# A fused four-layer image kernel: a shorter chain in the scan, fewer products in the global mixer, mode mixing with the modes stationary, and pieces of the output moved between two stages

## What is computed

```python
# layer 0: a = rfft2(x)[:, :, :32, :32];  two blocks of modes, each mixed over the 64 channels by complex weights
blk1 = _complex_matmul_2d(a, fw1)      # einsum bixy,ioxy->boxy, fw1 and fw2 of shape (64, 64, 32, 32, 2)
blk2 = _complex_matmul_2d(a, fw2)
out = irfft2(out_ft);  return relu(out @ W + b + out)
# layer 1: channels 0..31 windowed attention, channels 32..63 the global mixer, then a projection
fre = rfft2(xc); amp = abs(fre); pha = angle(fre)
amp_fea = amp * amp_w + amp_b;  pha_fea = pha * pha_w + pha_b
out = abs(irfft2(complex(amp_fea * cos(pha_fea) + 1e-08, amp_fea * sin(pha_fea) + 1e-08) + 1e-08))
# layer 2: the 16 x 16 lowest modes of fftn mixed, and back
# layer 3: for each of 1024 masked points the best context point by cosine, then a scan in raster order
def step(prev, inp):                   # prev: (8, 256) here
    mn, bst, mx = inp
    prev_n = prev / (norm(prev) + EPS)
    d_ad = maximum(sum(mn * prev_n), 0.0)
    cur = (d_ad * prev + mx * bst) / (d_ad + mx + EPS)
    return cur, cur
```

## Time and profile before

| what | us |
|---|---|
| median of 3 runs (lowest, highest) | 16272.47 (16264.12, 16278.23) |
| the profiled execution's own time | 16263.63 |
| its span in the trace | 16261.9 |
| mix_modes0 | 608 to 1287 |
| global_mixer with its last store | 6171 to 9204 |
| point_rows | 11751 to 12300 |
| select_points | 12303 to 13225 |
| coherent_scan | 13230 to 15920 |

### The profile page before, as it was taken

The page is one execution under the profiler, slowest core; times in us unless marked ns, Lnnn a source line. Parts: engine busy times, 40 slices in busy tenths (PEclk is TensorE's granted clock), DMA queues, the critical chain, the costliest instruction groups (busy, mean ns, idle before and its releaser), DMA issues. The chain is left out here.

```text
span 16261.9 us, 298044 instructions
## 1 busy us (share of the span) xinstructions
PE 11005.2 (68%) x109058; PEld 8114.0 (50%) x109058; DVE 9523.5 (59%) x20093; ACT 7395.5 (45%) x13170; POOL 4376.3 (27%) x3172
## 2 busy tenths in 40 slices
PE   8696667999999997999999899867715940000002
PEld 3493224777777776888888788532212410000001
DVE  3113445777777775666666433244465668888883
ACT  5211224777777774555554322433313544444440
POOL 0002344565655651111111255200005730000001
PEclk9757888999999998999999999988857975555555
DMA  6676673111111110111111499978896620000007
GB/s 258 174 145 203 215 243 115 41 43 39 42 42 42 42 42 31 61 44 42 52 53 42 145 363 364 325 238 358 364 376 206 183 76 9 10 10 9 10 10 290
DMA packets 1289991, 2177.92 MB, mean 134 GB/s; under 512 B 98836, under 2 KB 941988, under 8 KB 1221668
## 3 DMA queue, kind: packets, MB, share of 16 engines
q1 hardware_dynamic: 853124, 1613.43, 29.9%
q10 hardware_dynamic: 415008, 488.75, 9.2%
q0 software_dynamic: 20608, 58.22, 1.3%
HBM read 1370.06 MB, written 790.14 MB: 133 GB/s over the span
## 5 line engine op out<-in xcount | busy, mean ns | idle before, releaser
L731 POOL TENSOR_TENSOR la_s<-la_s,la_mx 128x512 f32<-128x512 f32 x2048 | 2094.3, 1044 | 1457.0 <-DVE la_mx L690 1456.7
L1928 PE MATMUL fp_tp<-fp_idn,fp_f 128*128 128x128 f32 x512 | 89.4, 344 | 2967.4 <-DMA fp_f<-ft 2950.0
L1928 PEld LDWEIGHTS fp_tp<-fp_idn,fp_f 128*128 128x128 f32 x512 | 77.8, 180 | 2979.6 <-issue 2761.2
L770 ACT ACTIVATE la_et<-la_pt 128x512 f32<-128x512 f32 x2048 | 1118.8, 600 | 737.6 <-PE la_pt L602 737.6
L602 PE MATMUL la_pt<-la_idn,la_s 128*128 128x128 f32 x8192 | 1152.0, 285 | 219.7 <-POOL la_s L731 219.2
L690 DVE TENSOR_REDUCE la_mx<-la_s 128x16 f32<-128x1024 f32 x1024 | 1243.6, 1215 | 17.7
L682 DVE TENSOR_TENSOR la_s<-la_ps,la_post 128x2048 f32<-128x2048 f32 x512 | 1168.4, 2282 | 31.5 <-PE la_ps L588 31.3
L602 PEld LDWEIGHTS la_pt<-la_idn,la_s 128*128 128x128 f32 x8192 | 904.2, 144 | 335.4 <-issue 235.3
L1801 ACT ACTIVATE cs_junk<-cs_num 8x256 f32<-8x256 f32 x1024 | 427.0, 417 | 1323.9 <-DVE cs_num L1862 1090.5
L895 PE MATMUL gm_xp<-gm_fws,gm_y 128*128 128x258 f32 x4096 | 962.8, 389 | 52.8 <-ACT gm_ri L968 52.8
L1232 PE MATMUL pj_pp<-pj_pw,pj_at 128*128 128x256 f32 x4096 | 926.4, 379 | 0.0
(11 more groups left out here) (272 smaller groups left out, 27499.7 us busy)
## 6 DMA issues: line engine op xcount, KB each, us to landing
f_xt<-in_x SPq DMA_DIRECT2D x128, 1024.0 KB, 8.0
i_xr<-in_x SPq DMA_DIRECT2D x64, 2048.0 KB
x<-pj_o SPq DMA_DIRECT2D x64, 2048.0 KB, 10.1
f_xt<-x SPq DMA_DIRECT2D x128, 1024.0 KB, 13.8
i_xr<-x SPq DMA_DIRECT2D x64, 2048.0 KB, 14.4
x<-i_xo ACTq DMA_DIRECT2D x64, 2048.0 KB, 14.5
mx_fw<-in_L_conv_fw SPq DMA_DIRECT2D x32, 2048.0 KB
x1l<-i_xo ACTq DMA_DIRECT2D x128, 512.0 KB, 10.7
```

The lines of the kernel that those rows point to most:

```text
L731: nc.gpsimd.tensor_tensor(sv, sv, mb, ALU.subtract).then_inc(s_sub, 1)
L770: nc.scalar.activation(et[:, k % RT].rearrange("p h n -> p (h n)"), t_bank(S, i)[:, :, :].rearrange("p h n -> p (h n)"), ACT.Exp).then_inc ...
```

## The change

The four parts are independent of each other.

**1. `EARLY` 8 to 3.** point_rows keeps 6 pieces an image, select_points gets 18; nothing else in the two functions changes.

```diff
-EARLY = 8
+EARLY = 3
```

```diff
-    NK = 2
...
+    NK = 4
...
+                def load(t):
...
+                    for half, src in zip(halves, (fw1, fw2)):
+                        for q in range(3):
+                            sp.dma_start(a[half, j, q, :, :], modes[:, q, :, kx].rearrange("b i n -> i b n")).then_inc(s_a[j], 16)
+                        sp.dma_start(fw[half, j, :, :], src[:, :, t * NK:(t + 1) * NK, :, :].rearrange("i o x y r -> i o (x y r)"))\
...
+                def mix(n):
...
+                    for s in range(SLOTS):
+                        for r in range(2):
+                            for g in range(G):
...
+                                for f, half in enumerate(halves):
+                                    last = nc.tensor.matmul(mp[g * 32:g * 32 + M, n % 2, f, s * C:(s + 1) * C],
+                                                            a[half, j, 1 - r:3 - r, :, x * NM0 + ky].rearrange("p q b -> p (q b)"),
+                                                            fv[half, :, x, ky, r], start=(r == 0), stop=(r == 1))
...
+                def turn(n):
...
+                            last = nc.tensor.matmul(tz[n % 2][half, s * G * M:(s + 1) * G * M],
+                                                    zs[:, n % 2, f, s * C:(s + 1) * C], sel[:, :], start=True, stop=True)
...
-                                    last = nc.tensor.matmul(mp[n % 2][f][half, ky * 2 * B:(ky + 1) * 2 * B],
-                                                            fv[half, :, x, ky, r], rhs, start=(r == 0), stop=(r == 1))
...
+                    mix(n)
...
+                        turn(n - 1)
...
+                        rotate(n - 2)
```

```diff
-    LAG = 2
+    LAG = 3
...
-                        for k in range(4):
-                            wh, q = k // 2, k % 2
...
+                    for q in range(2):
+                        for wh in range(2):
+                            last = nc.tensor.matmul(xp[c % 2][q][:, :], y[:, c % 2, wh, q * P:(q + 1) * P], fws[:, q, wh, :],
...
-                        for k in range(4):
-                            s, q = k // 2, k % 2
...
+                    for blk, pair in enumerate((((sr, 0), (di, 1)), ((si, 0), (dr, 1)))):
+                        for k, (z, mat) in enumerate(pair):
...
+                def half_sample(b, c):
...
+                    nc.scalar.activation(ri[0:1, g % 2, 2 * i + 1, 0, :], src[0:1, NF:2 * NF], ACT.Copy)
+                    nc.scalar.activation(ri[0:1, g % 2, 2 * i + 1, 1, :], src[0:1, 0:NF], ACT.Copy, scale=-1.0).then_inc(s_fix, 1)
...
+                def scale_amplitudes(b, k):
...
+                        last = nc.scalar.activation(v, v, ACT.Identity, scale=aw[:, c:c + 1], bias=ab[:, c:c + 1])
...
+                def combine(b, c):
...
+                    nc.vector.scalar_tensor_tensor(plus, xp[c % 2][1][:, :], sg[:, 0:1], minus, ALU.mult, ALU.add)
+                    nc.vector.scalar_tensor_tensor(minus, xp[c % 2][1][:, :], sg[:, 1:2], minus, ALU.mult, ALU.add).then_inc(s_xe, 1)
...
+                def signs(b, k, ch):
...
+                    dve.wait_ge(s_z, b * NG + k)
...
+                def fold(b, g, first):
...
+                    nc.gpsimd.tensor_tensor(sr[:, j, :, :], cp[:, :, 0:K], cm[:, :, 0:K], ALU.add).then_inc(s_fold, 1)
+                    nc.gpsimd.tensor_tensor(si[:, j, :, 0:K - 1], sp_[:, :, 1:K], sm[:, :, 1:K], ALU.add)
...
+                    nc.gpsimd.tensor_tensor(di[:, j, :, :], sm[:, :, 0:K], sp_[:, :, 0:K], ALU.subtract).then_inc(s_fold, 1)
+                    nc.gpsimd.tensor_tensor(dr[:, j, :, 0:K - 1], cp[:, :, 1:K], cm[:, :, 1:K], ALU.subtract)
...
+                    nc.gpsimd.tensor_scalar(sr[:, j, :, :], sr[:, j, :, :], 4e-8, None, ALU.add)
+                    nc.gpsimd.tensor_scalar(si[:, j, :, 0:K - 1], si[:, j, :, 0:K - 1], 2e-8, None, ALU.add)
...
+                    nc.gpsimd.tensor_tensor(di[0:1, j, :, :], cp[0:1, :, 0:K], cm[0:1, :, 0:K], ALU.subtract)
+                    nc.gpsimd.tensor_tensor(dr[0:1, j, :, 0:K - 1], sp_[0:1, :, 1:K], sm[0:1, :, 1:K], ALU.subtract)
```

```diff
+    UNROLL = 8
...
-        rs = m.sb("rs", [B, 2])
+        rs, dd = m.sb("rs", [B, 2]), m.sb("dd", [B, 2])
...
-        NCHAIN = 8
+        NCHAIN = 7
...
+            @block.sync
...
+                        load(n + 2)
...
+                            act.wait_ge(s_e1, step + 1)
+                            nc.scalar.activation(y[:, i, :], num[:, i, :], ACT.Copy, scale=sm[:, i, 2:3]).then_inc(s_y, 1)
...
-                            nc.vector.tensor_scalar(e2, e1, r, None, ALU.mult).then_inc(s_ch, 1)
...
-                            nc.vector.tensor_scalar(d, e2, inverse, None, ALU.mult).then_inc(s_ch, 1)
-                            dve.wait_ge(s_cur, step + 1)
...
-                            nc.vector.scalar_tensor_tensor(num[:, o, :], num[:, i, :], d, mbt[:, j, k, :],
+                            nc.vector.scalar_tensor_tensor(num[:, o, :], y[:, i, :], inverse, mbt[:, j, k, :],
...
-                            nc.vector.reciprocal(rs[:, o:o + 1], den).then_inc(s_rs, 1)
```

More of the change, by code:

```diff
@@ L339, in _ @@
+                load(0)
+                for half in halves:
                     sp.dma_start(wi[half, :], wmat).then_inc(s_const, 16)
                     sp.dma_start(eyes[half, :], eye).then_inc(s_const, 16)
[L341 to L345 removed]
@@ L940, in body @@
-                        if g >= LAG:
-                            inverse(b, g - LAG)
-                        elif not first:
-                            inverse(b - 1, g - LAG + NG)
+                            c = g * GC + i
+                            columns(b, c)
+                            if back:
+                                inverse_rows(*back, i)
+                            if c + 2 < HALF:
+                                rows(b, c + 2)
+                            if back:
+                                inverse_columns(*back, i)
@@ L1013, in inverse_copies @@
+                copy_o(b, NG - LAG, 2)
+                copy_o(b, NG - LAG, 3)
+                for g in range(NG - LAG + 1, NG):
                     copy_u(b, g, 0)
@@ new lines, in _, with ratio @@
+                s, c_ = (q[:, :, :, :].rearrange("p i s k -> p (i s) k") for q in (ps, pc))
+                def ratio(b, k, ch, first):
+                    dve.wait_ge(s_abs, b * (2 * NG) + 2 * k)
+                    if k != 1 or not first:
+                        dve.wait_ge(s_prod, b * (2 * NG) + (2 * k - 2))
+                    ch.step(nc.vector.scalar_tensor_tensor(t2, t0, TINY, t1, ALU.max, ALU.max))
+                    ch.step(nc.vector.reciprocal(t4, t2))
+                    ch.step(nc.vector.tensor_tensor(t3, t0, t1, ALU.min))
+                    ch.step(nc.vector.tensor_tensor(t0, t1, t0, ALU.is_gt))
+                    nc.vector.tensor_tensor(t3, t3, t4, ALU.mult).then_inc(s_ratio, 1)
@@ new lines, in body @@
+                def body(b, first):
+                    for g in range(NG):
+                        c, chain = g * GC, g > 0 or not first
+                        ch = Chain(dve, s_ch, b * (NG * NS) + (g - 1) * NS)
+                        if g:
+                            combine(b, c)
+                        if chain:
+                            ratio(b, g, ch, first)
+                        if not g:
+                            combine(b, c)
+                        if chain:
+                            signs(b, g, ch)
+                        combine(b, c + 1)
+                        if chain:
+                            angle(b, g, ch)
+                        combine(b, c + 2)
+                        if chain:
+                            amplitude(b, g)
+                            phase(b, g, ch)
+                            assert ch.n == NS
+                        combine(b, c + 3)
+                        zero(b, g)
+                        if chain:
+                            products(b, g)
@@ L1120, in _ @@
+                dve.sem_inc(s_sign, 2)
+                scales(0)
+                for_images(dve, body)
+                b, k = B - 1, NG
+                ch = Chain(dve, s_ch, b * (NG * NS) + (k - 1) * NS)
+                ratio(b, k, ch, False)
+                signs(b, k, ch)
+                angle(b, k, ch)
+                amplitude(b, k)
+                phase(b, k, ch)
+                products(b, k)
             @block.gpsimd
@@ L1813, in _, with current @@
-                with act.Fori(0, NL // 2 - 1) as t:
-                    for j in range(2):
-                        batch(t * 2 + j, j, True)
-                for j in range(2):
-                    batch(NL - 2 + j, j, False)
-                for j in range(2):
-                    act.wait_ge(s_store[j], (NL // 2) * 16 + 16)
+                def current(step, i, j, k):
+                    act.wait_ge(s_rs, step + 1)
+                    nc.scalar.activation(go[:, j, k, :], num[:, i, :], ACT.Copy, scale=rs[:, i:i + 1]).then_inc(s_cur, 1)
@@ L1821, in _ @@
```

(1 more changed line is left out.)

667 lines of the change are left out of this document (386 added, 281 removed).

## The result

The changed kernel takes 15213.59 us (median of 4 runs, 15206.63 to 15218.25) against 16274.34 (4 runs, 16264.12 to 16278.23): a ratio of 0.9348, interval 0.9337 to 0.9359. That is 1061 us faster, where 1362 was forecast: inside the range, 300 above the forecast. The profiled execution has a span of 15214.5, so its terms can be read against the 16261.9 of before. These two spans differ by 1047; the medians differ by more because the profiled execution of before lay 11 under its median.

The account below looks back on a forecast made before the run. Bounds before: TensorE in the mixer, transfers in point_rows, VectorE's dependent chain in the scan, no engine full in select_points. 16263.6 - 584 (scan) - 533 (mixer) - 262 (mix_modes0) + 20 (EARLY) = 14905, median 14910; range 14720 to 15250.

Parts of the forecast that it names:

- y ends near 1.91, num may start at 1.95: Scan step: ScalarE's y ends about 1.91 us after num, next num possible at 1.95; step taken as 2.01 us.
- The 0.04: Scan: the us left between the end of ScalarE's y (1.91) and the start of the next num (1.95).
- The rival of the step that stays at 2.31: Scan: ScalarE's y comes later and num waits, step stays 2.31 us, +307, total 15220; chance 0.08.
- The rival of the loop's code: Scan: long loop body fetched anew each turn, each instruction costs its fetch; at 210 ns total 16,500; chance 0.01.
- the rival of strided weights: mix_modes0: strided weight reads or non-overlapping column tiles make mixing 14.5 us a row, no gain, total 15180; chance 0.12.
- The penalty for each new line of 16 bytes: mix_modes0: SBUF accesses crossing to a new line pay, weights' columns lying 1 KB apart; no price given.
- 229 GB/s at share 0.77, so 297 at full: mix_modes0: mix_modes2's DMA rate, scaled to full share, applied to 67.1 MB of weights, giving 226 us.
- The near-tie that I called hidden: mix_modes0: DMA's 350 to 378 us runs beside PE's 371, stage forecast at 423 us.
- the edge of its 13: Mixer: GpSimd's fold, forecast 11 to 12 us, stays hidden up to 13; each us above costs 64.
- the rival of 40 to 42: Mixer: a group takes 40 to 42 us through slow fold or engines in lockstep, total 15230 or 15360; chance 0.15.
- the "15" of uncovered ends: point_rows: 15 us of work at the ends, formerly hidden by DMA, shows; stage goes from 549 to 336.
- the forecast case's own range: Whole kernel: 14750 to 15080 us for the forecast case, chance 0.62.

## Why the prediction was right or wrong

**Direction and kind: right.** All four parts act in the direction forecast, and the stages' new bounds are those named for the mixer (VectorE and its turn, 35 us a group) and for select_points (POOL busy 1018 of 1163, forecast 1024 of 1155).

**Scan, -584 forecast, -444 measured.** The step that failed is "y ends near 1.91, num may start at 1.95": y to num takes 0.70, not 0.54, since VectorE starts 0.19 behind the end of the ScalarE instruction it waits for. The step became 2.11 and not the 2.01 taken, 0.10 x 1024 = 102 us. VectorE's own path was forecast at 1.99 and is 2.06, by the operation with two operands; so even an exact y would have left some 50 of these 102. The 0.04 was what ScalarE needs behind VectorE; the other way I had no row and left it so. The other 38 are turns of the loop and batch ends, for which I had 48 us where 87 stand. The rival of the step that stays at 2.31 named the right wait and the wrong size. The rival of the loop's code named a true cost, of 5.9 us at the turn and not in every instruction.

**mix_modes0, -262 forecast, -105 measured.** The matmuls came out as forecast (5.5 us for 6, turn and rotate 4.2 for 5.6), and the rival of strided weights is refuted: the matmul group is busy 176 us where that rival wanted 464. The penalty for each new line of 16 bytes, which the prediction took from the Trainium skill ("SBUF - State Buffer", section "Door 1: The DMA port swizzle"), does not show in this group (21.5 ns a row). Two other steps failed. First, "229 GB/s at share 0.77, so 297 at full" and the 226 us for the weights from it: this rate of mix_modes2 did not carry over. The weights' packets of 1 KB took 84 ns (median) here and 46 there, and by their sum they held the 16 engines for 339 us; modes and `zd` took 67 and 69, as forecast. All of it, 96.6 MB, took 458 us in the run with half of the products, 211 GB/s. Why the packets are slower, no run tells. Secondly, the sum counted matmuls and bytes but not TensorE's instructions, which the faster matmuls now wait for: 187 us of "issue", 97 of it gone without most of the weights' loads. The near-tie that I called hidden (PE 371, DMA 350 to 378) was the place to doubt: two streams, each near the length of the stage and coupled by a double buffer, came to 580 where the runs with most of one left out took 446 and 458.

**Mixer, -533 forecast, -484 measured.** The fold took 13.1 us, on the edge of its 13; the signs did not wait for it. What failed is that its length was the only cost counted: on two of VectorE's products it took 1.5 us a group, 96 us, while both engines read SBUF. Without that cost regular groups take 34.0, a microsecond under the forecast 35, so part of the closeness is two errors that cancel. Since groups still averaged 38.0 with the images' turns (forecast 37.3), the rival of 40 to 42 did not come.

**EARLY, +20 forecast, -19 measured.** select_points is right to 1 us. In point_rows the "15" of uncovered ends did not appear, and the transfers ran at 395 GB/s, 1.02 of the engines, not 368.

**The range** held the result, at its upper end; the forecast case's own range, to 15080, did not. The scan and mix_modes0 erred the same way: in both I priced each engine by its busy time alone and the hand-over between engines, or between an engine and the queue, at next to nothing.
